# A graph network on one Trainium2 core: how the bias rows of the next table are issued

## The reference

```python
for i in range(3):                                  # L0, GCN
    h = segment_sum(norm * (h @ W)[src], dst) + b   # + self loops
    h = batchnorm(relu(h + x0))
x = layernorm(x + h)
x = layernorm(x + eve(eve(x)))                      # L1: x @ Wself.T + eve @ Weve.T + bias
x = layernorm(x + sage(swish(sage(x))))             # L2: mean @ Wl.T + b + x @ Wr.T
x = layernorm(x + gat(x))                           # L3
```

## Time and profile before

| | us |
|---|---|
| time before, median of 3 runs | 10869.92 |
| lowest and highest of them | 10861.84, 10874.02 |
| span of the profiled execution | 15443.7 |
| `deg` in the profile, about | 100 to 890 |
| `m0`, `m1`, `m2` in the profile, starts at about | 890, 2553, 4240 |
| `n3`, from about | 5935 to 6495 |
| `m4`, `m5`, `m6`, `m7` in the profile, starts at about | 6495, 8153, 10037, 11524 |
| `g8`, from about | 13199 to the end |

### The profile page before, as it was taken

One profiled execution on the slowest core, in us unless ns is written; L12 is line 12 of the kernel. 1 busy time (PEld: TensorE's weight loads), 2 busy tenths in 40 slices (PEclk: granted clock), 3 DMA queues, 4 the chain that ended last, 5 costly groups with the idle time before them and its releaser, 6 DMA issues. The chain is left out here.

```text
span 15443.7 us, 165743 instructions
## 1 busy us (share of the span) xinstructions
PE 7253.9 (47%) x36946; PEld 5501.8 (36%) x36947; DVE 6203.1 (40%) x16108; ACT 4646.1 (30%) x8631; POOL 7180.1 (46%) x7582
## 2 busy tenths in 40 slices
PE   1024544454534448854455555533334445445553
PEld 0024444444534444333333333323333333223332
DVE  3333433343434335522222333322223333378887
ACT  1111111111211114422222333412223333266676
POOL 4654444444454441144444444355554444557663
PEclk9987777777767779977777777866666667667776
DMA  6965554666656667644444444545555555233333
GB/s 164 209 154 171 172 167 148 205 200 194 202 176 198 193 194 255 235 142 158 143 166 143 162 160 159 177 144 173 168 171 170 183 177 192 81 104 119 114 114 100
DMA packets 1864962, 2570.76 MB, mean 166 GB/s; under 512 B 255901, under 2 KB 1369141, under 8 KB 1864662
## 3 DMA queue, kind: packets, MB, share of 16 engines
q1 hardware_dynamic: 1134168, 1627.20, 32.9%
q10 hardware_dynamic: 504726, 564.87, 11.2%
q0 software_dynamic: 225792, 375.94, 8.7%
HBM read 1499.55 MB, written 1129.98 MB: 170 GB/s over the span
## 5 line engine op out<-in xcount | busy, mean ns | idle before, releaser
L1078 POOL DMA_INDIRECT sums_gcn<-m_result,m_idx x1176 | 1162.8, 989 | 2311.9 <-DVE m_result L1399 1952.8
L1220 ACT ACTIVATE m_nodeT<-m_n_bank 128x512 f32<-128x512 f32 x980 | 544.3, 597 | 4220.6 <-remote 2400.8
L1626 PE MATMUL m_gram<-m_y 128*128 128x129 f32 (+1 forms) x4800 | 900.6, 336 | 1765.6 <-issue 1462.9
L1683 DVE SCALAR_TENSOR_TENSOR m_acc<-m_n_bank,m_scales,m_res_b 128x128 f32<-128x128 f32 (+1 forms) x2352 | 644.9, 343 | 2569.6 <-remote 1864.2
L1078 POOL DMA_INDIRECT sums_eve<-m_result,m_idx x784 | 762.7, 973 | 1696.8 <-DVE m_result L1515 1470.9
L1187 PE MATMUL m_n_bank<-k_ident,m_in_y 128*128 128x128 f32 x5488 | 895.6, 321 | 1310.0 <-DVE m_z L1772 826.9
L1772 DVE TENSOR_TENSOR m_z<-m_n_bank,m_in_sums 128x512 f32<-128x512 f32 (+1 forms) x784 | 511.9, 687 | 2412.8 <-remote 1300.2
L1626 PEld LDWEIGHTS m_gram<-m_y 128*128 128x128 f32 (+1 forms) x4800 | 801.2, 245 | 1845.4 <-issue 1523.6
L1078 POOL DMA_INDIRECT sums_sage<-m_result,m_idx x784 | 762.7, 973 | 1375.9 <-DVE m_result L1399 1134.3
L1070 POOL DMA_INDIRECT m_rows<-node_rows_a,m_idx x1176 | 1124.4, 956 | 358.5 <-issue 338.1
L1187 PEld LDWEIGHTS m_n_bank<-k_ident,m_in_y 128*128 128x128 f32 x5488 | 754.1, 168 | 1437.8 <-DVE m_z L1772 902.7
(11 more groups left out here) (302 smaller groups left out, 17415.1 us busy)
## 6 DMA issues: line engine op xcount, KB each, us to landing
m_in_sums<-sums_gcn SPq DMA_DIRECT2D x291, 512.0 KB
m_in_y<-node_rows_a SPq DMA_DIRECT2D x291, 512.0 KB
sums_gcn<-k_gcn_b SPq DMA_DIRECT2D x194, 512.0 KB
node_rows_a<-m_y ACTq DMA_DIRECT2D x194, 512.0 KB
m_in_x<-in_x_dram SPq DMA_DIRECT2D x194, 512.0 KB
m_in_y<-node_rows_b SPq DMA_DIRECT2D x194, 512.0 KB
sums_eve<-k_eve_b SPq DMA_DIRECT2D x194, 512.0 KB
m_in_sums<-sums_eve SPq DMA_DIRECT2D x194, 512.0 KB
```

What stands on the lines that cost most here:

```text
L1078: pool.indirect_dma_start(self.node_sums[:, :], bass.IndirectOffsetOnAxis(self.idx[s][:, T + t:T + t + 1], 0), self.result[b][:, t, :], No ...
L1220: act.activation(out, src, ACT.Copy).then_inc(self.n_turn_read, 1)
L1626: mm = pe.matmul(self.gram[:, 0:D + 1], self.y1[b][0:rows[b], t, 0:D], self.y1[b][0:rows[b], t, :], start=False, stop=False, skip_group_ch ...
L1683: ins = dve.scalar_tensor_tensor(out=self.acc[b][0:n, tt, :], in0=ph.node_out(i, n)[:, t, :], scalar=self.scales[b][0:n, tt:tt + 1], in1=s ...
```

## The change

SyncE no longer issues fills in `load_nodes`. A new method `fill_program` issues them all: the table of 100,000 rows is cut into four parts, each part is one transfer on 125 partitions with 200 rows of 512 B each (12.8 MB), from the bias row on 125 partitions repeated by a stride of 0. ScalarE calls it as the first thing of its program in each of the seven convolutions. `all_filled`, still on SyncE at the end, waits for 4 transfers in place of 98. The bytes and the rows are the same. `deg` and `g8` are not touched.

```diff
+FILL_P, FILL_PIECES = 125, 4
...
+    def fill_program(self, eng):
         if self.fill_table is not None:
-            for b in range(2):
-                c = m * 2 + b
-                n = self.sh.rows(c)
-                sp.dma_start(node_rows(self.fill_table, c, self.sh),
-                             spread_slots(self.fill_row[0:n, :], [n, T, D])).then_inc(self.filled, 16)
+            rows = self.sh.n // (FILL_P * FILL_PIECES)
+            table = self.fill_table.rearrange("(s p j) f -> s p j f", p=FILL_P, j=rows)
+            for s in range(FILL_PIECES):
+                eng.dma_start(table[s], spread_slots(self.fill_row[0:FILL_P, :], [FILL_P, rows, D])).then_inc(self.filled, 16)
 
     def all_filled(self, sp):
         if self.fill_table is not None:
-            sp.wait_ge(self.filled, 16 * self.sh.node_chunks)
+            sp.wait_ge(self.filled, 16 * FILL_PIECES)
...
         @block.scalar
         def _(act):
+            ph.fill_program(act)
             merged_sweep(act, k, sh, lambda *u: edges.scalar(act, *u), lambda *u: nodes.scalar(act, *u))
```

More of the change, by code:

```diff
@@ L57, in __init__ @@
         self.last_nodes = n_nodes - (self.node_chunks - 1) * CH
-        assert self.last_nodes % T == 0 and n_nodes < FAR
+        assert self.last_nodes % T == 0 and n_nodes < FAR and n_nodes % (FILL_P * FILL_PIECES) == 0
         self.last_rows = self.last_nodes // T
```

## The result

The changed kernel takes 13857.9 us (median of four runs, 13827.7 to 13866.0) against 10865.9 us for the kernel before on the same chip (10860.5 to 10874.0): a ratio of 1.2746, 95% interval 1.2728 to 1.2764, or +2992 us. The forecast was 13264 us.

A forecast was written before the change was run, and what follows sets the result against it. Stages were taken as chains of turns, SyncE waiting on ScalarE's copies, no engine or DMA full. Per stage 430 - 88 = 342 us, seven stages 2394; 10869.9 + 2394 = 13264 us, range 12000 to 14900.

The forecast's parts named there:

- signs named: If right: seven stages 250 to 550 us longer each, 20 small packets per stage, degrees, norm and GAT unchanged.
- the store wait of the third pair: ScalarE blocks in `out_free` for pair 2 until the fill drains: 430 us per stage; this case's chance 0.62.
- Five engines: Each 125-partition fill transfer runs on 5 DMA engines, not 16, adding 5 marks; 20 small packets per stage.
- The drain: At stage start, 20,000 packets per engine at 28.3 ns, 566 us, plus about 50 other: ends about 616 us.
- The start of the third pair: ScalarE reaches the third node pair about 185 us after the stage's start, at the earliest after 110 us.
- The saving: Fills leave SyncE's FIFO in the node loop: bounds 0 and 177 us per stage, half taken, 88.
- The rival that the issue blocks: Fill issues hold ScalarE: five stages with ScalarE edge work lose 528 us each, two SAGE stages 342; 14194 us, chance 0.27.
- The rival that 16 engines make it a win: All 16 engines share the opening fill, drained in 227 us; 47 to 136 us per stage gained, 10541 us, chance 0.08.
- break-even at 12.6 engines: Engine count where the fill's added wait equals the 88 us saved; 13 or more make a win, fewer a loss.

The follow-up runs named there:

- 80 x 1: Changed kernel with the fill as one transfer of 80 partitions x 1250 rows by ScalarE at the stage's start: 12153.2 us, ratio 1.1165.
- 80 x 5: Changed kernel with the fill as five transfers of 80 partitions x 250 rows, same place and queue: 12257.6 us, ratio 1.1257.
- 100 x 4: Changed kernel with the fill as four transfers of 100 partitions x 250 rows: 12938.5 us, ratio 1.1893.
- 125 x 4: The changed kernel itself: four transfers of 125 partitions x 200 rows by ScalarE at the stage's start, 13857.9 us, ratio 1.2746.
- 125 x 4 by SyncE: Changed kernel with the same four transfers issued by SyncE ahead of its first edge pair, not by ScalarE: 13960.6 us, ratio 1.2833.

## Why the forecast was right, and where it was off

The direction held, and so did the root of the loss: the fill runs on five engines, and ScalarE cannot go on until most of it has drained. Of the signs named, the stages came 370 to 507 us longer, with 20 small packets each, and degrees, norm and GAT were unchanged. But the place where ScalarE stands is not the one forecast. Its first long hold is not the store wait of the third pair but 369 us in the fill's own issues, which is the sign that the prediction gives for its rival. Of the 409 us by which the third pair of m0 is late, 330 are there at the first pair already (404 us after the beginning in place of 73); only 79 are added at the stores. That the forecast's price came near all the same rests on the hold and the store wait lying over the same drain, as the run with one transfer showed on 16 engines; on five engines no such run was made.

The size was built from two terms per stage, 430 us of wait less 88 us saved, and both were off: 342 us forecast, 2942 / 7 = 420 us measured.

*Five engines* (right): 20 marks per stage, as counted. The Trainium skill, "DMA: Bandwidth & Descriptors", section "Why a DMA increments its semaphore by 16 and not by 1", has the rule (the largest number up to 16 that divides the slowest dimension of both sides); for 125, 100 and 80 partitions it comes to 5, 10 and 16, and the marks of all three agree.

*The drain* (too long): 28.3 ns per packet was taken, from 16 engines, and 23.5 measured on five (35 ns on ten and 40 on 16 with such long transfers). The third pair started at 522 us, not at 616.

*The start of the third pair* (too late): 185 us came from the stretched execution; in an undisturbed one it is 113. The forecast named 110 as the earliest possible. The two errors nearly cancel, which is luck: 522 - 113 = 409 us of delay instead of 430.

*The saving* (the step that failed): half of 177 us per stage was taken off, because fills stood ahead of loads and stages looked like chains of turns with nothing full. That reading came from an execution 42% too long. In an undisturbed one the queue wait of the earlier trace rows is not the limit; GpSimd is, back to back for 996 of 1022 us in m4, and the fills were hidden. Their removal costs 181 us over the seven stages (26 each) instead of saving 616.

With the two measured terms the sum is 7 x 409 + 181 = 3044 us, against 2942 for the stages. The same sum serves the other kernels with an early fill, from the third pair of m0 alone:

| fill at the start | third pair, us late | 7 x that + 181 | measured, stages |
|---|---|---|---|
| 80 x 1 | 159 | 1294 | 1265 |
| 80 x 5 | 175 | 1406 | 1385 |
| 100 x 4 | 283 | 2162 | 2056 |
| 125 x 4 | 409 | 3044 | 2942 |
| 125 x 4 by SyncE | 435 | 3226 | 3078 |

It is 1.5 to 5% high throughout: the stages win a little back, chiefly m4 to m7 (m4 loses 370 us where m0, with its 409 us of delay, loses 400).

*The rival that the issue blocks* was right on the fact. ScalarE was held 369 us, against the forecast's reading of the earlier trace rows, where a few short transfers were accepted ahead of earlier ones. Its price was wrong: it let the stages whose edges need ScalarE lose 528 us and the SAGE stages 342, and m4 and m6 lose 370 and 374, so the edge work behind the hold is no extra loss. (m1 and m2 lose 504 and 507, but some 100 us of that each is the removal's, as above.) The hold lies inside the wait that comes anyway: about 15 us per stage, by the run with one transfer (on 16 engines). Its 14194 us, with the same drain and saving, still lies nearer to the measured 13858 us than the 13264 us of the forecast.

*The rival that 16 engines make it a win* (10541 us) would have been wrong even had its condition been met: 12258 us with 16 engines in use. Its drain of 227 us was near the measured 250; its saving, which was to pay for that, does not exist, and so there is no break-even at 12.6 engines. The room in the opening was room on the engines, not in ScalarE's queue, through which both the fill and the first stores had to go.

The rule to coalesce many small transfers (the Trainium skill, "DMA: Bandwidth & Descriptors", "Rules for kernel authors") was set beside that rival. Here the packets keep their 512 B, and a larger transfer was not faster: the fill alone took 1764 us in pieces of 10.2 MB and 1506 us in pieces of 410 KB (one run). Small transfers, which the rule is about, no run here has.

No version beat the kernel before. The stages are bound by GpSimd's indirect DMAs, and in m5 more likely by TensorE, by the 25 us above; with 16 engines, how the fill is cut and spread behind the pairs changes the time by 0 to 0.6%.

## What to carry to other kernels

Before reading who is the limit, set the profile's span beside the timed runs; where it is 42% longer, waits and shares describe that execution and not the kernel. A transfer moved to a quiet place still stands ahead of whatever next uses its queue: look for the first issue, store or load behind it, and charge the whole drain, at the rate of the engines that the shape uses. And work that hides behind the limiting engine is worth nothing when removed; it may even be what keeps loads and stores apart.

## What the hardware showed unasked

- An issue of the fill on ScalarE or SyncE returned at once (0.70 to 0.97 us) when no large transfer was ahead in its queue, even for 100,000 rows, and was otherwise held until the one ahead has about drained (117.6 us at 5000 packets per engine, 87.4 at 2500, 49.6 at 1250).
- 512 B packets from one repeated row did not speed up in proportion to the engines: 109 GB/s on five, 202 to 206 on sixteen in pieces of 20,000 rows, 238 on sixteen in pieces of 800 rows.
- GpSimd's indirect DMAs followed each other every 1.27 us at the closest, 0.97 us each and 0.3 us between.
